# Attention followed by a recurrent scan: GpSimd adds all four blocks of exponentials, one product for a step's sums, and the products are dealt out anew around the scores

## The reference, cut to what matters

```
xn = rms_norm(x) * (1 + scale) + shift          # scale, shift = cond @ W_emb + b_emb
q, k, v = xn @ W_qkv ; q = rms_norm(q) ; k = rms_norm(k)
attn = softmax(q @ k.T * d ** (-0.5))
o = attn @ v ; x = x + o + o @ W_out
x = x + GRU(cond, x)                             # 512 steps, one after the other
x = x + conv(x) ; x = x + conv(x) + b
```

## Time and profile before

| | us |
|---|---|
| median of 3 runs | 2163.62 (2162.48 to 2163.7) |
| the profiled execution, its own time | 2165.77 |
| its span, first to last instruction | 2164.0 |
| PE busy, share of the span | 2091.8, 97% |
| DVE busy | 1384.6, 64% |
| ACT busy | 1174.7, 54% |
| POOL busy | 1128.8, 52% |
| mean granted clock of TensorE | 0.994 |

### The profile page before, as it was taken

How to read it: one execution, slowest core, us unless ns; L and a number is a source line. 1 busy time by engine, 2 the same in 40 slices (tenths; PEclk the granted TensorE clock), 3 DMA queues, 4 the chain that set the end, 5 groups by cost and what they waited for, 6 DMA issues and landing times.

```text
span 2164.0 us, 183094 instructions
## 1 busy us (share of the span) xinstructions
PE 2091.8 (97%) x76192; PEld 1575.2 (73%) x76192; DVE 1384.6 (64%) x5127; ACT 1174.7 (54%) x5995; POOL 1128.8 (52%) x3891
## 2 busy tenths in 40 slices
PE   7999999999999999999999999999999999999997
PEld 2222222222389999999999999999999999998886
DVE  3343444444267777777777777777777777777775
ACT  3445445443255555555555555555555555555555
POOL 0143332333146666666666666666666666666665
PEclk9999999999999999999999999999999999999999
DMA  6000000001122222222222121222121212210001
GB/s 253 2 1 1 1 2 1 1 21 60 36 63 52 54 52 52 52 54 51 67 54 57 48 55 49 58 59 65 49 57 49 56 47 62 64 32 6 5 7 19
DMA packets 217582, 95.89 MB, mean 44 GB/s; under 512 B 170120, under 2 KB 213384, under 8 KB 216712
## 3 DMA queue, kind: packets, MB, share of 16 engines
q1 hardware_dynamic: 217272, 92.53, 16.3%
q10 hardware_dynamic: 208, 2.13, 0.3%
HBM read 26.30 MB, written 12.58 MB: 18 GB/s over the span
## 4 chain that ended last, share of the span: by engine, by line
PE 63%; DVE 8%; issue 1%; POOL 0%; DMA 0%; SPq 0%; POOLq 0%; ACT 0%; DVEq 0%
PE ps L1162 57%; DVE arena L1011 5%; PE ps L1190 4%; PE ps L1201 2%; DVE arena L1017 1%; DVE arena L1023 1%; DVE arena L1028 1%; DMA arena<-arena 0%; POOL arena L1234 0%; SPq L939 0%; POOL arena L1238 0%; POOL arena L1240 0%; POOL arena L1244 0%; POOL arena L1247 0%; POOL seq L1250 0%
## 5 line engine op out<-in xcount | busy, mean ns | idle before, releaser
L1162 PE MATMUL ps<-whh,arena 128*4 128x128 f32 (+1 forms) x65536 | 1448.2, 246 | 36.8 <-DVE arena L1028 32.8
L1162 PEld LDWEIGHTS ps<-whh,arena 128*4 128x4 f32 x65536 | 1300.3, 87 | 142.9 <-DVE arena L1028 64.5
L1011 DVE STREAM_TRANSPOSE arena<-ps 128x128 f32<-128x128 f32 x1024 | 436.6, 426 | 226.3 <-PE ps L1162 226.1
L1120 ACT ACTIVATE arena<-arena 128x8 f32<-128x8 f32 x1024 | 215.8, 211 | 637.2 <-DVE arena L1011 637.0
L1234 POOL TENSOR_TENSOR arena<-tap,seq 128x32 f32<-128x32 f32 x1024 | 232.1, 259 | 216.5 <-DVE seq L1041 216.5
L427 DVE TENSOR_REDUCE top<-ps 128x2 f32<-128x1024 f32 x128 | 150.7, 1219 | 253.1 <-PE ps L683 253.1
L1028 DVE TENSOR_TENSOR_SCAN arena<-arena 128x24 f32<-128x24 f32 x1024 | 213.8, 209 | 145.1 <-ACT arena L1131 145.1
L1095 ACT ACTIVATE ps<-arena 128x128 f32<-128x128 f32 x1026 | 269.7, 263 | 0.4 <-PEq L206 0.4
L1234 POOL TENSOR_TENSOR arena<-tap,arena 128x32 f32<-128x32 f32 x1024 | 232.2, 259 | 66.8 <-POOL arena L1244 66.8
L1017 DVE STREAM_TRANSPOSE arena<-ps 128x64 f32<-128x64 f32 x1024 | 257.5, 252 | 12.6 <-PE ps L1162 2.6
L264 POOL TENSOR_TENSOR arena<-arena 128x2048 f32<-128x2048 f32 x16 | 72.8, 4548 | 352.1 <-ACT arena L337 352.1
(11 more groups left out here) (90 smaller groups left out, 1386.8 us busy)
## 6 DMA issues: line engine op xcount, KB each, us to landing
arena<-arena SPq DMA_DIRECT2D x216, 114.0 KB, 2.2
arena<-arena SPq DMA_DIRECT2D x112, 128.0 KB, 2.2
arena<-seq SPq DMA_DIRECT2D x224, 55.0 KB, 2.0
arena<-gi_d SPq DMA_DIRECT2D x248, 32.0 KB
gi_d<-arena SPq DMA_DIRECT2D x96, 57.0 KB
seq<-in_x SPq DMA_DIRECT2D x4, 1024.0 KB, 17.6
out<-seq SPq DMA_DIRECT2D x14, 256.0 KB
whh<-in_w_hh SPq DMA_DIRECT2D x1, 3072.0 KB, 21.6
```

What stands on the lines that cost most here:

```text
L1011: e.transpose(trn[:, h].rearrange("p q (i c s) -> p q c i s", c=2, s=2)[:, :, :, :, 0], bank[RN[h]][:, 0:P].rearrange("p (q c i) -> p q c ...
L1120: e.activation(r_d0[:, h].rearrange("p (i s) -> p i s", s=2)[:, :, 1], trn[:, h, 0, 0:2 * NH].rearrange("p (i s) -> p i s", s=2)[:, :, 0], ...
L1162: last = e.matmul(bank[dst[h]][32 * G:32 * G + B, 0:n], hv, wv[:, k, gates, G, 64 * h:64 * h + 64], start=False, stop=k2 == 1 and k == C - ...
```

## The change

POOL adds block 3 as well (`add_last`), in all steps but the last, so `sums` is one quad instead of two. A buffer of exponentials is given free by POOL's adds and `weigh` alone. `weigh` and `sums` come later: slot j of step n holds `weigh` of two blocks back (`weigh_late`), and the sums of step n - 1 stand in slot 1 of step n instead of slot 0. In the loop, gaps A and B of every slot are filled anew; `norm(0)` stands ahead of `scores(n + 1, 2)`, `sums_x` in gap B of slot 0; gap A of slot 2 holds `weigh`, one quad of `tile_x` and `norm(1)`, and gap B of slot 3 two quads of `tile_x` and `turn_tops`. On ACT `invert` moves behind the first exponentials and `keep(0)`, `rms_x` ahead of `keep(0)`, and `squares_x` to the end of the step before. On DVE `heads_out` moves behind the second maxima, and in step 15 `take(3)` stands ahead of it.

```diff
--- before.py
+++ after.py
@@ -264,9 +264,14 @@
                     e.tensor_tensor(acc, pT[:, (4 * n) % NPT], pT[:, (4 * n + 1) % NPT], ALU.add).then_inc(g_acc, 1)
 
                 def add_third(n):
-                    wait(g_acc, 2 * n + 1)
+                    wait(g_acc, 3 * n + 1)
                     wait(a_exp, 8 * n + 6)
                     e.tensor_tensor(acc, acc, pT[:, (4 * n + 2) % NPT], ALU.add).then_inc(g_acc, 1)
+
+                def add_last(n):
+                    wait(g_acc, 3 * n + 2)
+                    wait(a_exp, 8 * n + 8)
+                    e.tensor_tensor(acc, acc, pT[:, (4 * n + 3) % NPT], ALU.add).then_inc(g_acc, 1)
 
@@ -278,6 +283,8 @@
                     if has_x(n):
                         add_shift(n // 4 + 1)
                     add_third(n)
+                    if n + 1 < NS:
+                        add_last(n)
 
             @block.scalar
             def _(e):
@@ -328,10 +335,7 @@
                     if i >= NPT:
                         e.wait_ge(p_pv, i - NPT + 1)
                         m, k = divmod(i - NPT, 4)
-                        if k < 3:
-                            e.wait_ge(g_acc, 2 * m + (2 if k == 2 else 1))
-                        else:
-                            e.wait_ge(p_sum, m + 1)
+                        e.wait_ge(g_acc, 3 * m + max(k, 1))
                     for h in range(2):
                         e.wait_ge(p_st, 2 * i + h + 1)
                         e.activation(pT[:, i % NPT, 2 * h:2 * h + 2].rearrange("p g t -> p (g t)"),
@@ -368,17 +372,15 @@
                     tops(n)
                     if has_v(n - 1) and n:
                         values(n - 1, 1)
-                    if n:
-                        invert(n - 1)
                     exponentials(n, 0)
                     if n == 0:
                         values(-1, 1)
                     if has_x(n):
-                        squares_x(n // 4 + 1)
+                        rms_x(n // 4 + 1)
                     if n + 2 < NS:
                         keep(0, n + 2)
-                    if has_x(n):
-                        rms_x(n // 4 + 1)
+                    if n:
+                        invert(n - 1)
                     exponentials(n, 1)
                     if n + 2 < NS:
                         keep(1, n + 2)
@@ -389,6 +391,8 @@
                     if has_v(n):
                         values(n, 0)
                     exponentials(n, 3)
+                    if has_x(n + 1):
+                        squares_x((n + 1) // 4 + 1)
                 invert(NS - 1)
                 e.preload_act_table_set("sigmoid_and_others")
                 e.wait_ge(p_pv, 4 * NS)
@@ -520,10 +524,13 @@
                         maxima(n + 1, 0)
                     if has_out(n - 1):
                         add_out(n - 1, 1)
+                    if n + 1 < NS:
+                        maxima(n + 1, 1)
+                    if n + 1 == NS:
+                        take(3)
                     if n:
                         heads_out(n - 1)
                     if n + 1 < NS:
-                        maxima(n + 1, 1)
                         if n + 2 == NS:
                             take(0)
                         maxima(n + 1, 2)
@@ -542,7 +549,7 @@
                         norm(1, n + 2)
                     if has_out(n):
                         add_out(n, 0)
-                for u in range(3, len(UNIT)):
+                for u in range(4, len(UNIT)):
                     take(u)
                 heads_out(NS - 1)
                 for b in range(B - 1):
@@ -582,7 +589,7 @@
                     if b == 0:
                         e.wait_ge(d_const, 4)
                     else:
-                        e.wait_ge(a_lsum, 4 * (b - 1) + 1)
+                        e.wait_ge(a_top, 4 * (b - 1) + 2)
                     for k in range(C):
                         e.wait_ge(a_xsq, C * b + k + 1)
                         product(bank[SS], ones[:], xsq[:, k], k == 0, k == C - 1).then_inc(p_xs, 1)
@@ -628,8 +635,6 @@
                         e.wait_ge(a_ln[1], 1)
                     else:
                         e.wait_ge(a_rx, 1)
-                    if n >= 3 and s == 0 and has_x(n - 2):
-                        e.wait_ge(a_rx, 2 * ((n - 2) // 4 + 1) + 1)
                     e.wait_ge(a_sq[s], n + 1)
                     product(bank[SS], onesb[:], sqb[:, s], True, True).then_inc(p_norm[s], 1)
 
@@ -777,13 +782,24 @@
 
                 def sums(n):
                     e.wait_ge(a_top, min(n + 2, NS))
-                    e.wait_ge(g_acc, 2 * n + 2)
-                    for last_block in range(2):
-                        src = pT[:, (4 * n + 3) % NPT] if last_block else acc
+                    if has_x(n + 1):
+                        e.wait_ge(a_rx, 2 * ((n + 1) // 4 + 1) + 1)
+                    e.wait_ge(g_acc, 3 * n + (3 if n + 1 < NS else 2))
+                    terms = [acc] if n + 1 < NS else [acc, pT[:, (4 * n + 3) % NPT]]
+                    for i, src in enumerate(terms):
                         for g in range(NG):
-                            last = e.matmul(bank[SS][32 * g:32 * g + 32], ones[:, 0:32], src[:, g], start=not last_block,
-                                            stop=bool(last_block))
+                            last = e.matmul(bank[SS][32 * g:32 * g + 32], ones[:, 0:32], src[:, g], start=i == 0,
+                                            stop=i + 1 == len(terms))
                     last.then_inc(p_sum, 1)
+
+                def weigh_late(n, j):
+
+                    if j >= 2:
+                        weigh(n, j - 2)
+                    elif n:
+                        weigh(n - 1, j + 2)
+                        if j:
+                            sums(n - 1)
 
                 e.wait_ge(d_const, 4)
                 e.wait_ge(l_vec, 16)
@@ -814,73 +830,54 @@
                 value_tile(-1, 0, range(C))
                 turn_tops(0)
                 for n in range(NS - 2):
-                    more, ahead = n + 1 < NS, n + 2 < NS
-                    if more:
-                        scores(n + 1, 0)
-                    if n:
-                        weigh(n - 1, 3)
-                        sums(n - 1)
+                    scores(n + 1, 0)
+                    weigh_late(n, 0)
+                    project(0, n + 2, range(0, 2))
                     shifted(n, 0)
                     if n == 0:
                         value_tile(-1, 1, range(C))
-                    if ahead:
-                        project(0, n + 2, range(0, 3))
-                    if more:
-                        scores(n + 1, 1)
-                    if ahead:
-                        project(0, n + 2, range(3, 4))
-                    weigh(n, 0)
+                    project(0, n + 2, range(2, 4))
                     if has_x(n):
                         sums_x(n // 4 + 1)
-                    if ahead:
-                        project(1, n + 2, range(0, 1))
+                    project(1, n + 2, range(0, 1))
+                    scores(n + 1, 1)
+                    weigh_late(n, 1)
+                    project(1, n + 2, range(1, 2))
                     shifted(n, 1)
-                    if ahead:
-                        project(1, n + 2, range(1, 4))
-                    if more:
-                        scores(n + 1, 2)
-                    if ahead:
-                        norm(0, n + 2)
-                    weigh(n, 1)
+                    project(1, n + 2, range(2, 4))
...
                 n = NS - 2
                 for j in range(4):
                     scores(n + 1, j)
-                    if j == 0:
-                        weigh(n - 1, 3)
-                        sums(n - 1)
-                    else:
-                        weigh(n, j - 1)
+                    weigh_late(n, j)
+                    if j:
                         gates(5 * j - 2, 5 * j)
                     shifted(n, j)
                     gates(5 * j, 5 * j + 3)
                 turn_tops(n + 1)
                 n = NS - 1
                 for j in range(4):
-                    if j == 0:
-                        weigh(n - 1, 3)
-                        sums(n - 1)
-                    else:
+                    if j:
                         gates(16 + 5 * j, 19 + 5 * j)
-                        weigh(n, j - 1)
+                    weigh_late(n, j)
                     shifted(n, j)
                     if j < 3:
                         gates(19 + 5 * j - (j == 0), 21 + 5 * j)
                 gates(34, C * len(UNIT))
+                weigh(n, 2)
                 weigh(n, 3)
                 sums(n)
                 for c in (2, 3, 0, 1):
```

More of the change, by code:

```diff
@@ L825, in _ @@
                         value_tile(-1, 1, range(C))
-                    if ahead:
-                        project(0, n + 2, range(0, 3))
-                    if more:
-                        scores(n + 1, 1)
-                    if ahead:
-                        project(0, n + 2, range(3, 4))
-                    weigh(n, 0)
```

(36 more changed lines are left out.)

## The result

The changed kernel takes 2174.3 us (median of 6 runs, 2172.51 to 2174.47) against 2164.89 of the kernel before, run beside it (median of 6, 2162.48 to 2167.61). The ratio is 1.0041, 95% interval 1.0031 to 1.0052: slower by 0.4%. Forecast were 2150.9 us and a range of 2146 to 2158.

What follows compares the result with a forecast made beforehand. PE's products were taken to bound full attention steps, with each slot's circle of scores, shifted and exponentials as the other bound. Terms -8.3, -2.6, -3.6 and +1.8 gave -12.7 us, so 2150.9 us, range 2146 to 2158.

Steps and rivals of the forecast that it cites:

- The scan behind is the same code and gets nothing: The scan after the attention: code unchanged, so no change of time was counted for it.
- Full steps: Steps 3 to 13 of the attention: 0.75 us less each for the removed quad, -8.3 us over eleven steps.
- The circle of slot 3: Slot 3 of full steps: the chain scores, shifted, exponentials, next scores ends last, by some 0.1 us over the products.
- the two waits for POOL: PE's waits for POOL at the sums behind steps 5 and 9, 1.45 and 1.18 us: both go, -2.6 us.
- The covers that I costed at nothing: Full steps: the moved work of POOL, ACT and DVE stays hidden behind other work, at no cost.
- rival C: Sums behind steps 1, 5 and 9: POOL's fourth add is too late, the waits stay, 2155.5 us; chance 10%.
- Steps 0 to 2: First attention steps: +0.3 us in step 1 and -3.9 in step 2, sum -3.6 us, bounds +2 and -8.
- rival D: First steps run without a slow clock stretch, or step 15 without its wait: 2146.5 us; chance 10%.
- Steps 14 and 15: Last attention steps: -0.2 and +0.6 us in step 14, a 1.4 us wait in step 15, sum +1.8 us.
- the wait for the take: Step 15: PE waits 1.4 us ahead of gates(24, 26) for DVE's take(4), queued behind heads_out(14).
- Rival B: The clock falls at every step's boundary, 1.8 us each, eleven costing 20 us: slower, 2171 us; chance 5%.
- an overlooked stall: Anywhere in the kernel: a stall the prediction missed, no size given; chance 3%.

Runs made afterwards that it cites:

- e1: The changed kernel with 19 idle semaphore instructions on POOL ahead of its scan loop; 2152.01 us, ratio 0.9950 to the kernel before.
- e13: The changed kernel with 10 idle semaphore instructions on POOL ahead of its scan loop; 2198.4 us, ratio 1.0156 to the kernel before.
- e12: The changed kernel with POOL's scan loop written out twice and four idle semaphore instructions more for each pair of time steps; 2210.0 us, ratio 1.0215.
- e6: The changed kernel without POOL's two convolutions during the scan, its loop only counting its semaphore; 2147.29 us, ratio 0.9922.
- e9: e1 with sums back at two quads at its new place, both multiplying acc; 2164.05 us, ratio 1.0003 to the kernel before.

## Why the prediction was wrong

**The step that failed** is one sentence of the sum: "The scan behind is the same code and gets nothing." The code is the same, its place is not. The change adds 15 adds with their waits on POOL, 45 instructions, and that moves POOL's loop across the border. The term stood at nothing and measured +22.8 us, which no part of the change costs by itself. I had weighed POOL's adds only where they stand. The trace had POOL at 52% of the span, and I did not ask how near its loop in the scan was to the recurrence it runs beside. It was near: a pair of steps takes 6.05 us, and POOL's own work and gaps in it, without the one at the start, 6.14 - 0.76 = 5.38; any gap above 0.67 (0.69 by the traces with pairs of 6.12) makes POOL the slower of the two. At 0.76 it is, by 0.09 us a pair: 256 x 0.09 = 23 us, against 2174.3 - 2152.0 = 22.3 between the changed kernel and e1.

One small part of the 22.8 is something else. The granted clock was 0.50 from 586.0 to 589.4 us, and the first 128 products of the scan took 4.39 us; in e1, with the same wait of 2.2 us ahead of them and the clock at 1.00, they took 2.83.

How DVE comes to follow POOL's pace, with nothing in the code that waits for POOL, is to be seen at the scan's beginning. POOL's first add of a pair follows the end of DVE's sum by 0.26 us at 603.56 us, then by 0.34 at 609.71, 0.44 at 615.85, by 0.43 to 0.46 from 634 to 1967 us, and by 0.33 to 0.35 from 1979 us on. In the kernel before it is 0.26 in most pairs, so there POOL waits for DVE each time; in the changed kernel it does not. POOL falls back until its adds meet DVE's scans, and they then hold DVE up. In the changed kernel, L1241 an add of POOL and L1025 a scan of DVE:

```profile
1003.94 0.21 DVE L1025 TENSOR_TENSOR_SCAN arena<-arena 128x24 f32<-128x24 f32 x1
...
1004.80 0.26 POOL L1241 TENSOR_TENSOR arena<-seq,arena 128x32 f32 x1 [0.27 <-POOL arena L1237]
1004.86 0.26 DVE L1025 TENSOR_TENSOR_SCAN arena<-arena 128x24 f32<-128x24 f32 x1 [0.28 <-ACT arena L1128]
```

The scan that begins 0.06 us behind POOL's add ends 0.06 behind its end, and takes 0.26 us; the one before it took 0.21. The same holds for all scans that begin within an instruction of POOL, between 700 and 1900 us: a scan of L1025 ends after its usual 208 ns or 61 ns behind the end of that instruction, whichever is later, and one of L1020 after 192 ns or 47 ns behind it. That gives the length of all but one of the 1562 scans of the changed kernel to 0.012 us. In the kernel before, 1046 scans begin within an instruction of POOL too, but all but two of them so late in it that its end comes too soon to matter. (The Trainium skill, "SBUF — State Buffer", section "SBUF: two separate sides", says that a VectorE instruction with two inputs in SBUF and a GpSimd instruction take the port they share by turns, each for its whole length. These lengths agree: the scan is held until POOL's instruction has ended.)

Four scans of each line in a pair, 17 ns longer each, are 0.13 us, enough for the 0.09 by which the pair grew. In e13 the lag settles at 0.53 us and L1020 takes 257 ns. In e12, with POOL's pace at 6.29, DVE's pairs last 6.13 and POOL falls behind for good; that the meetings can pass on no more is my reading. That the meetings are the link is inferred from lag, scan lengths and e6; no run moved the meetings alone.

**Full steps**, forecast -0.75 each: measured 31.35 - 30.67 = -0.68. The circle of slot 3 does end last. The 0.07 too much were in the prediction's own sum: it had `scores` start "at most 0.14" behind 221.23 and took 221.3; with the whole 0.14, which is what was measured, it would be 222.05 - 221.37 = 0.68. Steps 3 to 13 lasted 354.81 us and last 344.32: -10.5, with the two waits for POOL, against -8.3 - 2.6 = -10.9. That part was right, and e9 confirms the price of a quad where the products end last, 0.86 against 0.87.

**The covers that I costed at nothing** all held: the only wait of PE between 150 and 505 us is one of 0.4 us of `shifted` for DVE's maxima, and none names POOL, `norm`, `heads_out` or `squares_x`. The sums behind steps 1, 5 and 9 don't wait (against rival C).

**Steps 0 to 2**: -6.4 (152.97 against 159.34), forecast -3.6 with -8 as bound. The clock fell behind PE's waits in step 0 and at its end (twice, between 80 and 92 us) and from 115 to 118.5 us, and all of that lies before step 2: step 2 is a full one of 30.68 us where 33.5 were forecast, and step 1 35.2 instead of 34.9. It is rival D's direction.

**Steps 14 and 15**: the wait for the take is 1.28 us against 1.4. From S14 to the scan 88.79 us against 86.22, +2.6, forecast +1.8. Step 14 is +0.4, as forecast. The missing 0.8 is at the scan's start, where PE now waits 2.23 us for ACT instead of 1.22; the prediction had no term for it.

**Rival B**, a clock that falls at each boundary, which was my only way to "slower", didn't happen: 1.00 in all full steps, PE busy 29.89 of 30. Past 150 us the clock left 1.00 only at the scan's start, as said above, and at the very end. The time came out near B's 2171 for another reason, for which I had only the 3% of an overlooked stall.

## What to carry to other kernels

When a change adds or removes instructions on an engine's queue, every loop behind them on that queue moves, and its rounds can become longer: here the gap at the start of POOL's loop grew by 0.10 or 0.18 us, while moving PE's loops by 4 or 60 instructions changed nothing. Before calling a later stage untouched, look for engines whose loop is nearly as long as the loop it runs beside: in the trace, an engine that is "released" by another after a gap near its own shortest. Writing such a loop out two or four times makes the way back rarer; here both were as fast as the best place, though each was run at one place only. And read a change's traces stage by stage before judging it: here a gain of 14 us was hidden by a loss of 23 that moving one loop mends.

## What the runs showed of the hardware that was not expected

The gap at the start of POOL's loop has three lengths for the same 46 instructions, 0.66, 0.76 and 0.84 us, by where the loop stands; shifts by 64 and 75 instructions were fast, by 32, 45, 48 slow, by 55 slowest. The slow loops are those that hold one fixed place of the program: their way back takes 0.257 us instead of 0.162, and one instruction at that place comes 0.08 to 0.09 us late. An idle semaphore instruction on POOL took 0.078 us. Two engines that have no semaphore from the one to the other can fall into step, by all that is seen through their meetings in SBUF: DVE took POOL's pace of 6.14 (and 6.23) us a pair, but not 6.29.
